# Half of the weighted products folded before TensorE sums them, and every engine's pieces in another order

## The reference

```python
for c in range(CIRCUITS):                                   # 4
    scores = jnp.abs(mod) ** 2 * SCALING                    # (b, s, i, j): 8x8 per token
    amps = jnp.sqrt(jax.nn.softmax(scores, axis=-1) + 1e-12)
    weighted = jnp.einsum('bsij,bsjd->bsid', w, vq)         # w: amps with a sign
    amp = jnp.clip(jnp.abs(co), ERR_MIN, 1.0)
    final = final + sup_w[c] * corrected
return measured @ W_out.T + b_out
```

## Time and profile before

| | |
|---|---|
| median of 3 runs | 2515.89 us (2506.96 to 2516.02) |
| profiled execution | 2518.26 us, its span 2516.5 us |
| mean granted TensorE clock | 0.897 |
| busy share of the span | PE 79%, DVE 77%, POOL 54%, ACT 50% |
| first to last execution of L635 | 96.2 to 1968.3 us, 32 executions |

### The profile page before, as it was taken

One profiled execution on the slowest core, in us unless ns is written; L12 is line 12 of the kernel. 1 busy time (PEld: TensorE's weight loads), 2 busy tenths in 40 slices (PEclk: granted clock), 3 DMA queues, 4 the chain that ended last, 5 costly groups with the idle time before them and its releaser, 6 DMA issues. The chain is left out here.

```text
span 2516.5 us, 43496 instructions
## 1 busy us (share of the span) xinstructions
PE 1978.0 (79%) x14556; PEld 1538.8 (61%) x14556; DVE 1928.1 (77%) x3471; ACT 1262.5 (50%) x2982; POOL 1360.5 (54%) x1106
## 2 busy tenths in 40 slices
PE   1478888888888888888888888888888836758699
PEld 0466666666666666666666666666666624647477
DVE  8989899999988999989989888999998511512223
ACT  2256555555555555655655556666655413303132
POOL 5656666666666666666666666666663253142200
PEclk9889889999989999989998899999898857879799
DMA  3000000000000000000000000000000011020110
GB/s 93 5 5 10 9 8 8 8 8 8 10 8 10 8 10 8 10 8 8 8 8 8 8 8 8 8 8 8 8 6 7 5 38 36 11 67 14 54 34 26
DMA packets 64577, 39.56 MB, mean 16 GB/s; under 512 B 9350, under 2 KB 60431, under 8 KB 64528
## 3 DMA queue, kind: packets, MB, share of 16 engines
q1 hardware_dynamic: 60386, 30.51, 4.3%
q0 software_dynamic: 4096, 8.40, 1.2%
q10 hardware_dynamic: 46, 0.00, 0.0%
HBM read 26.31 MB, written 12.58 MB: 15 GB/s over the span
## 5 line engine op out<-in xcount | busy, mean ns | idle before, releaser
L774 PE MATMUL pa<-ident,arena 128*128 128x128 f32 x4096 | 530.7, 286 | 56.8 <-DVE arena L652 52.5
L774 PEld LDWEIGHTS pa<-ident,arena 128*128 128x128 f32 x4096 | 503.0, 201 | 74.0 <-DVE arena L652 35.3
L1059 PE MATMUL pb<-ident,arena 128*128 128x128 f32 x1536 | 290.6, 302 | 157.0 <-ACT arena L954 142.0
L1059 PEld LDWEIGHTS pb<-ident,arena 128*128 128x128 f32 x1536 | 187.6, 153 | 275.4 <-issue 187.6
L954 ACT ACTIVATE arena<-pb 128x384 f32<-128x384 f32 x512 | 252.5, 493 | 188.2 <-PE pb L1059 152.1
L680 POOL TENSOR_TENSOR arena<-state,c_cross 128x448 f32<-128x448 f32 x128 | 203.3, 1608 | 206.1 <-DVE state L541 201.3
L672 POOL TENSOR_TENSOR arena<-arena,neg_half 128x32 f32<-128x32 f32 x64 | 264.9, 4158 | 83.7 <-DVE arena L518 83.7
L652 POOL TENSOR_TENSOR arena<-arena 128x1024 f32<-128x1024 f32 x64 | 150.3, 2348 | 195.2 <-PE pa L774 195.2
L947 ACT ACTIVATE arena<-pd,arena 128x256 f32<-128x256 f32 x512 | 245.1, 479 | 0.0
L652 DVE TENSOR_TENSOR arena<-arena 128x1024 f32<-128x1024 f32 x192 | 235.9, 1254 | 2.6 <-PE pa L774 2.2
L946 ACT ACTIVATE arena<-pd,arena 128x128 f32<-128x128 f32 x512 | 188.8, 369 | 67.1 <-DVE arena L834 65.0
(11 more groups left out here) (250 smaller groups left out, 4403.0 us busy)
## 6 DMA issues: line engine op xcount, KB each, us to landing
x_land<-in_L_attn_query SPq DMA_DIRECT2D x32, 128.0 KB, 2.1
arena<-in_L_attn_query SPq DMA_DIRECT2D x32, 128.0 KB, 2.1
x_scratch<-x SPq DMA_DIRECT2D x32, 128.0 KB, 1.8
xn_scratch<-xn_d SPq DMA_DIRECT2D x32, 128.0 KB, 1.8
arena<-x_scratch SPq DMA_DIRECT2D x16, 256.0 KB
out_x<-arena SPq DMA_DIRECT2D x16, 256.0 KB
w<-in_L_ffn_W SPq DMA_DIRECT2D x1, 2048.0 KB
arena<-xn_scratch,arena POOLq DMA_INDIRECT x128
```

Source lines behind the costliest of these rows:

```text
L774: mm = pe.matmul(pa[:, t, c * P:c * P + P], wprod[:, k % NWP, j * 128:j * 128 + 128], ident[:, :], start=(j == 0), stop=(j == NH - 1))
L1059: mm = pe.transpose(pb[:, j * P:j * P + P], p_raw[:, s % 3, j * P:j * P + P], ident[:, :])
```

## The change

Products 2 and 6 on VectorE (`HALVED`) and 3 and 7 on POOL (`ON_POOL`) get one more instruction each: the upper 512 numbers of the product are added onto the lower 512, in place. TensorE sums these four with four matmuls instead of eight. VectorE's half adds, called **H2** and **H6** here, are pieces of their own, so stage C has 33 pieces on VectorE in place of 31. POOL's half adds, **H3** and **H7**, stand right behind P3 and P7 and wait for them. Before each norm of stage B, POOL also waits until ScalarE has read the scales of the one before. All four orders are new.

```diff
-DVE_C_STEPS = 19
+DVE_C_STEPS = 21
...
-POOL_ORDER = "A1C2B1A4C1B1A2C1D1C1D1"
-ACT_ORDER = "E7A1E1A1E3A1E5B1E4B1E3C1A1E2B1E3C1E3B1A1E2C1E6A1E1B1D1C1D1C1D2"
-PE_ORDER = "E4A1E1A1E6B1E4B1E7B1E2B1E3C1E1C1E1C1E1C1D1C1D1C1D1C2D2C2"
-DVE_ORDER = "C1A1C1A1C1B1C1E1B1E1C2A1E1C1A1C1E1C2E1C2A1C1E1A1C1B1C1B1A1C1E1A1C2B1C1B1C1E1B1A1C1A1C2B2A2C2A1D2C2D3C1A2C2D2A1D2A1C1"
+POOL_ORDER = "A1B1C2A5C2A1D1B1C1D1"
+ACT_ORDER = "E3A1E2A1B1E3A1E4B1E5B1E2C1A1E7C1E2A1E3B1E1C1E2A1E6D1C2D2B1D1"
+PE_ORDER = "E3A1E1A1E1B1E3B1E14B1E4B1E1C1E1C1E1C1E1C1D1C2D2C3D2C1"
+DVE_ORDER = "A1C1A1C1B1C1B1C2E1C1E1A1C1A1C1E1C2E1C2A1B1C1E1C1A1C2A1C1A1E1B1C1A1E1C1A1C1A1B1A1C1B1E1B1C3A1C1A1C2D2B1C1D3C2B1C2A2D2A1D1C1D1"
...
+                        if k in HALVED:
+                            yield from L(weighted(v, t, c))
+                            w = wprod[:, k % NWP, :]
+                            v.tensor_tensor(w[:, 0:512], w[:, 0:512], w[:, 512:1024], ALU.add).then_inc(S("a_wprod"), 1)
...
-                weighted(g, k // NC, k % NC).then_inc(S("a_wpool"), 1)
+                weighted(g, k // NC, k % NC).then_inc(S("a_wfull"), 1)
+                g.wait_ge(S("a_wfull"), 2 * b + n + 1)
+                w = wprod[:, k % NWP, :]
+                g.tensor_tensor(w[:, 0:512], w[:, 0:512], w[:, 512:1024], ALU.add).then_inc(S("a_wpool"), 1)
...
+                    n = NH // 2 if k in HALVED or k in ON_POOL else NH
...
+                if n or not (isinstance(b, int) and b == 0):
+                    g.wait_ge(S("b_xn"), 4 * b + 2 * n)
```

More of the change, by code:

```diff
@@ L621, in vector_c @@
                             v.wait_ge(S("a_wsum"), 8 * b + k - NWP + 1)
-                        weighted(v, t, c).then_inc(S("a_wprod"), 1)
+                        if k in HALVED:
+                            yield from L(weighted(v, t, c))
+                            w = wprod[:, k % NWP, :]
+                            v.tensor_tensor(w[:, 0:512], w[:, 0:512], w[:, 512:1024], ALU.add).then_inc(S("a_wprod"), 1)
+                        else:
+                            weighted(v, t, c).then_inc(S("a_wprod"), 1)
                     if k == 6:
@@ L648, in build @@
         ON_POOL = (3, 7)
+        HALVED = (2, 6)
         def weighted(eng, t, c):
@@ L772, in tensor_c @@
                         pe.wait_ge(S("a_wprod"), 6 * b + k - k // NC + 1)
-                    for j in range(NH):
+                    n = NH // 2 if k in HALVED or k in ON_POOL else NH
+                    for j in range(n):
                         mm = pe.matmul(pa[:, t, c * P:c * P + P], wprod[:, k % NWP, j * 128:j * 128 + 128], ident[:, :],
-                                       start=(j == 0), stop=(j == NH - 1))
+                                       start=(j == 0), stop=(j == n - 1))
                     mm.then_inc(S("a_wsum"), 1)
```

## The result

| | before | after |
|---|---|---|
| median of 4 runs | 2515.95 us (2506.96 to 2522.38) | 2641.16 us (2638.20 to 2643.76) |
| profiled execution, span | 2518.26, 2516.5 us | 2643.76, 2641.6 us |
| mean granted TensorE clock | 0.897 | 0.802 |

The ratio is 1.0507 (95% interval 1.0475 to 1.0539): 125 us slower, where 74 were forecast.

What follows compares the result with a forecast made beforehand. VectorE was taken as the bound at 60.4 us per iteration; work 52.1, new work 1.4, contention 7.45 and idle 1.9 gave 62.8, +74 us over 31 iterations, 2590 us; own range 2530 to 2640, 8 in 10 2475 to 2660.

Steps and rivals of the forecast that it cites:

- TensorE's 4 us: Main loop: halving four of eight weighted sums saves TensorE 4.0 us per iteration, worth only what it takes off VectorE's waits.
- rival 1: Main loop: VectorE's waits go and contention stays at 3.0 us; 58.4 us per iteration, 2454 us; chance 0.17.
- rival 2: Main loop: contention and idle together stay within 0.4 us of 6.9, so no change, 2516 us; chance 0.13.
- rival 4: Main loop: TensorE was the bound after all, and 4.0 us go in each iteration, 2392 us; chance 0.02.
- Contention after, 7.45 us: Main loop: VectorE and POOL operations reading SBUF hold each other up, 7.45 us per iteration in place of 3.0; bounds 5.3, 9.7.
- P3 arrives inside the run: POOL's product 3, waiting for the first weighted sum, meets VectorE's eight two-input operations in a row; 2.0 us contention per iteration.
- Idle after, 1.9 us: Main loop: VectorE's remaining waits per iteration, 1.9 us in place of 5.3; bounds 1.0 and 2.5.
- idle grown elsewhere instead: Sign of a wrong prediction: VectorE's idle before L660, L635 or L853 has grown, so the new order is late at TensorE.
- The other sign of being wrong: VectorE's half add, L545 and a weighted product run at 0.7, 1.1 and 1.2 us, so POOL is elsewhere then.
- Rival 3: Main loop: slower still by TensorE's low clock, 1.5 to 2 us more idle; 64.6 us per iteration, 2646 us; chance 0.16.
- VectorE's and POOL's new work: The half adds: VectorE's two take 1.4 us per iteration, bounds 1.2 and 1.6; POOL's two 1.15 us each.
- L587 beside POOL's powers: Main loop: L587 takes its usual 0.41 us in the middle of POOL's L672, so powers cost VectorE nothing.

Runs made afterwards that it cites:

- e10: Changed kernel with the last stage B product and maxima issued before VectorE's first weighted product, plus filler matmuls in stage E; ratio 1.051 to the kernel before.

## Why the prediction was right, and where its sum was not

- **What bounds the loop, and the sign.** TensorE's 4 us are not worth having for themselves in the kernel before: shown by the short sums alone (1.012). Slower was right, and rivals 1, 2 and 4 are out. The size is in part luck: contention was put too high and idle much too low, and the two errors nearly cancel (62.8 us per iteration against 64.6).
- **Contention after, 7.45 us.** This is a term that failed: 3.3 us by the durations. (By subtraction, 64.6 - 9.1 - 52.1 - 1.4, it is 2.0; the 1.3 between the two is unexplained.) Its mechanism is right, its size is not, even with the old orders: there VectorE is busy 4.0 us more per iteration, 1.4 of it work, so contention rises by 2.6, where 4.45 were forecast for the new ones. With the new orders the step "P3 arrives inside the run" came true only where w0 took the 2.0 us that I gave it. In most passes w0 needed 3.2 to 3.8 us with low clock in it, so P3 came when VectorE was waiting for w1 anyway. L550 and L608, which paid before, no longer do, and L545 little.
- **Idle after, 1.9 us.** 9.1 measured. I read TensorE's waits at full clock and gave 0.3 us to the low one. The forecast that idle before the clip would go was right, and that before L640 shrank; the test that I set, idle grown elsewhere instead, shows a new order that is late at TensorE. The other sign of being wrong, H2, 545 and W4 at 0.7, 1.1 and 1.2 us, is there in most passes too.
- **Rival 3.** It is the nearest in number (64.6 per iteration, 2646 us) and in mechanism: TensorE at 0.80 in place of 0.93. It got there by adding 1.8 us to a contention that did not come, so the number is in part luck. Not in its place, though: of some 27 us of low clock per pass 22 lie before w0 and 1.3 between w3 and the end of L792, where the rival had them; and TensorE is idle 16% of the loop, not 26%, since half speed fills the time. The Trainium skill ("TensorE: Matmul & The Clock Gate", section "Why this matters for your kernels") warns of idle gaps between bursts of matmuls. The trace agrees in part: the slow w0 stands close behind a gap of 2.37 us, but the same gap of 1.58 us is followed by full speed in one pass and by half speed in another.
- **VectorE's and POOL's new work.** H2 alone lasts 0.69 us (0.68 taken). H3 and H7 take 1.27 us at the shortest in the changed kernel and 1.60 in the median, up to 2.34 with contention; the estimate was 1.15.
- **L587 beside POOL's powers.** The row that the prediction cites, 1081.75, stands in the last 0.4 us of L672, not in the middle. The reading holds all the same: 25 times in the trace of the kernel before L587 lies wholly inside one L672 and takes 0.41 to 0.42 us.
- **What is shown, and what is not.** Shown within the trace of the changed kernel: two passes that agree for 21.7 us differ by 3.9 us ten microseconds later by the clock alone, and VectorE waits for it. Shown within one trace of `e10`: the same program takes 2.9 to 5.4 us more per iteration when TensorE is at 0.82 than at 0.93 to 0.99. The new orders bring most of the low clock (0.82 with them alone, 0.90 with the half adds alone). What starts the low stretches is open: gaps of equal length are followed by either speed, closing one gap and filling others gave 1.2 and 1.1 us, and both together less than either. A changed kernel held at full clock throughout was not reached.

## What to carry to other kernels

Folding a product to spare the matmul engine moves work onto two engines that, in these traces, wait for each other when both read large operands from SBUF: price an add there by what the other one does at that moment, 0.7 us free, up to 2.4 us beside a large operation. A hand-made order for one engine's bursts must be read at the clock that the matmul engine will be granted under it, with both speeds tried for each wait. When parts of a change are tested apart, expect that they do not add; here each alone was worse than both, one of them by little.

## What was not expected of the hardware

- One program (`e10`) has two rhythms: 59.4 to 62 us per iteration for five iterations and 64.9 for the rest, with the clock at 0.93 to 0.99 and at 0.82. The pattern, once taken, repeats to 0.1 us.
- Four kernels with different orders and different work settle at the same 64.85 us per iteration.
- Adding 66 or 33 small matmuls per sequence whose results nothing reads made the kernel before 0.7 and 0.65% faster (granted clock in the loop 0.95 in place of 0.93).
- The stretch behind the main loop takes 548 and 540 us in the first comparison and 411 to 422 on the chips of the experiments, while the changed kernel's loop takes the same in both. In the changed kernel's two traces TensorE is busy 399 and 377 us of it and idle for the rest. No run here looked for the reason.
